# Transposing activations two chunks at a time through one PSUM bank

## What is computed

```
layer(h):                       # twice, with weights of its own
    a    = softmax(h @ h.T / sqrt(D)) * adj ;  attn = a / (sum(a) + 1e-10)
    ctx  = (attn above diagonal) @ (h @ wl.T + bl) + diag(attn) * (h @ ws.T + bs)
         + (attn below diagonal) @ (h @ wr.T + br)
    h    = relu(layernorm(ctx, 1e-12) * g + beta)
y   = layernorm(x + layer(layer(x)))
out = layernorm(y + attention(y, adj, 12 heads, + 0.1 * adj on the scores, masked where adj == 0))
```

## Time and profile before

| | |
|---|---|
| median of 3 runs | 1866.24 us (1865.49 to 1866.89) |
| the profiled execution | 1864.76 us, its span 1863.0 us |
| mean granted TensorE clock | 0.977 |
| instructions | 39868 |

### The profile page before, as it was taken

One profiled execution on the slowest core, in us unless ns is written; L12 is line 12 of the kernel. 1 busy time (PEld: TensorE's weight loads), 2 busy tenths in 40 slices (PEclk: granted clock), 3 DMA queues, 4 the chain that ended last, 5 costly groups with the idle time before them and its releaser, 6 DMA issues.

```text
span 1863.0 us, 39868 instructions
## 1 busy us (share of the span) xinstructions
PE 1731.2 (93%) x13120; PEld 1633.3 (88%) x13120; DVE 1555.4 (83%) x5383; ACT 1267.5 (68%) x3036; POOL 652.9 (35%) x777
## 2 busy tenths in 40 slices
PE   4899999999999999999999999999999999999963
PEld 4799899999999999999999999899999999999952
DVE  4578889888888988888998888898888889888865
ACT  3466767676767776676767676676767776767644
POOL 1223333343333334343334333333434333433331
PEclk9899999999999999999999999999999999999975
DMA  5157666767666666766676776666666667677555
GB/s 156 29 106 149 127 130 131 145 135 147 145 122 132 136 143 141 150 134 125 132 144 139 143 144 124 129 137 145 138 151 136 123 135 140 138 143 144 115 116 116
DMA packets 550036, 247.65 MB, mean 133 GB/s; under 512 B 423100, under 2 KB 549832, under 8 KB 549832
## 3 DMA queue, kind: packets, MB, share of 16 engines
q1 hardware_dynamic: 538928, 231.91, 61.9%
q10 hardware_dynamic: 10904, 13.20, 2.1%
HBM read 56.25 MB, written 12.58 MB: 37 GB/s over the span
## 4 chain that ended last, share of the span: by engine, by line
PE 61%; DVE 24%; ACT 9%; issue 3%; DMA 1%; SPq 1%; ACTq 0%; POOL 0%; DVEq 0%; POOLq 0%
PE bank_w L384 33%; PE bank_m L384 10%; PE bank_u L384 6%; PE bank_o L384 4%; DVE halves L890 4%; DVE bank_s L885 4%; PE bank_s L384 4%; ACT normed L632 2%; ACT bank_s L683 2%; DVE stats_y L851 2%; ACT halves L692 2%; DVE hlrl L792 2%; DVE normed L848 2%; PE bank_t L401 2%; DVE attTl L797 1%
## 5 line engine op out<-in xcount | busy, mean ns | idle before, releaser
L683 ACT ACTIVATE bank_s<-bank_s,hmin 128x256 f32<-128x256 f32 x768 | 311.1, 445 | 129.8 <-DVE hmin L885 114.1
L885 DVE CUSTOM_DVE_ANT_0 bank_s<-bank_s,bias_adj 128x256 f32<-128x256 f32 x768 | 308.1, 446 | 40.7 <-PE bank_s L384 40.4
L890 DVE TENSOR_TENSOR halves<-bank_s,halves 128x512 f16<-128x512 f32 x384 | 262.3, 683 | 27.4 <-ACT halves L692 24.3
L692 ACT ACTIVATE halves<-bank_s 128x512 f16<-128x512 f32 x384 | 228.6, 596 | 4.2
L384 PE MATMUL bank_w<-w_graph0h,hT_ach 128*128 128x384 f32 x576 | 201.5, 350 | 10.3 <-DVE w_graph0l L745 6.0
L384 PE MATMUL bank_w<-w_graph1h,hT_bh 128*128 128x384 f32 x576 | 200.1, 347 | 0.0
L384 PE MATMUL bank_o<-v_parts,pT 128*128 128x99 bf16 (+1 forms) x3072 | 186.7, 204 | 12.6 <-DMA pT<-halves 9.3
L384 PE MATMUL bank_w<-w_graph0l,hT_ach 128*128 128x384 f32 x576 | 195.6, 340 | 0.0
L384 PE MATMUL bank_w<-w_graph0h,hT_acl 128*128 128x384 f32 x576 | 195.3, 339 | 0.0
L384 PE MATMUL bank_w<-w_graph1l,hT_bh 128*128 128x384 f32 x576 | 195.0, 339 | 0.0
L384 PE MATMUL bank_w<-w_graph1h,hT_bl 128*128 128x384 f32 x576 | 194.6, 338 | 0.0
(11 more groups left out here) (177 smaller groups left out, 5327.3 us busy)
## 6 DMA issues: line engine op xcount, KB each, us to landing
x_in<-in_x SPq DMA_DIRECT2D x64, 384.0 KB, 3.7
adj_in<-in_adj SPq DMA_DIRECT2D x96, 256.0 KB, 3.6
q_st<-qk_hi SPq DMA_DIRECT2D x256, 96.0 KB, 2.3
k_st<-qk_hi SPq DMA_DIRECT2D x256, 96.0 KB, 2.3
q_st<-qk_lo SPq DMA_DIRECT2D x128, 96.0 KB, 2.2
k_st<-qk_lo SPq DMA_DIRECT2D x128, 96.0 KB, 2.2
out<-result ACTq DMA_DIRECT2D x32, 384.0 KB, 3.8
pT<-halves SPq DMA_TRANSPOSE x384, 3.1
```

The costliest lines, as they stand in the source:

```text
L683: nc.scalar.activation(bank[:, i * S:(i + 1) * S], bank[:, i * S:(i + 1) * S], ACT.Exp, bias=hmin[:, i, k:k + 1], scale=-1.0).then_inc(s_p ...
L692: nc.scalar.activation(halves[:, k % SPLIT, :, 0, :], bank_s[k % 2][:, :].rearrange("p (i s) -> p i s", i=NT), ACT.Copy).then_inc(s_pt_hi, 1)
L885: ve.tensor_tensor_reduce(bank_s[k % 2][:, i * S:(i + 1) * S], bank_s[k % 2][:, i * S:(i + 1) * S], bias_adj[:, i, :], -SCALE, BIG, ALU.ad ...
L890: ve.tensor_tensor(halves[:, k % SPLIT, :, 1, :], bank_s[k % 2][:, :].rearrange("p (i s) -> p i s", i=NT), halves[:, k % SPLIT, :, 0, :], ...
```

## The change

The three tensors are turned in two steps in place of three: TURNS = ((0, 1), (2,)). Step 0 does chunks 0 and 1, four transposes that fill bank_t wholly; step 1 does chunk 2 with two transposes. For x and y ACT copies and DVE subtracts 512 columns in one instruction for step 0, 256 for step 1. For h ACT still makes two passes per chunk (its scale and bias differ by chunk), four for step 0, and then DVE subtracts 512 columns in one. All semaphore counts on these steps go from NC to len(TURNS). In the lists the first of the three steps goes away, the second becomes step 0, the third step 1, and the rest keeps its place: on PE `turn_y.0` stands ahead of `a_mix.0` and `turn_y.1` behind it, `turn_h.0` ahead of v.0 and `turn_h.1` between v.0 and v.1, `turn_x.0` behind `b_scores` and `turn_x.1` behind `b_proj.1`. The waits in a_x, b_x, a_scores, b_scores, a_proj, b_proj and qk change in their counts only, and they mean the same as before.

```diff
+TURNS = ((0, 1), (2,))
...
@@ -47,26 +48,26 @@
 ORDER = {
     "pe": """
         a_proj.2-1 scores.7-1 a_proj.3-1 attend.4-1 a_proj.4-1 a_proj.5-1 attend.5-1 scores.8-1 scores.9-1
-        turn_y.0-1 turn_y.1-1 a_mix.0-1 turn_y.2-1 attend.6-1 scores.10-1 a_mix.1-1 attend.7-1 q.0 q.1
-        scores.11-1 attend.8-1 q.2 k.0 attend.9-1 turn_h.0 k.1 k.2 turn_h.1 v.0 turn_h.2 v.1 attend.10-1
-        turn_x.0 attend.11-1 b_scores.0 turn_x.1 scores.0 scores.1 b_proj.0 b_proj.1 turn_x.2 b_proj.2
+        turn_y.0-1 a_mix.0-1 turn_y.1-1 attend.6-1 scores.10-1 a_mix.1-1 attend.7-1 q.0 q.1
+        scores.11-1 attend.8-1 q.2 k.0 attend.9-1 k.1 k.2 turn_h.0 v.0 turn_h.1 v.1 attend.10-1
+        attend.11-1 b_scores.0 turn_x.0 scores.0 scores.1 b_proj.0 b_proj.1 turn_x.1 b_proj.2
         scores.2 b_proj.3 b_turn.0 b_proj.4 b_proj.5 scores.3 scores.4 a_scores.0 b_mix.0 attend.0 scores.5
         attend.1 b_mix.1 a_proj.0 a_proj.1 attend.2 a_turn.0 scores.6 attend.3""",
     "act": """
         a_proj.2-1 scores.7-1 weights.6-1 a_proj.3-1 b_norm2.0-1 a_proj.4-1 weights.7-1 b_out.0-1 a_proj.5-1
-        turn_y.0-1 scores.8-1 turn_y.1-1 weights.8-1 scores.9-1 turn_y.2-1 weights.9-1 scores.10-1 q.0
-        h_norm.0 q.1 weights.10-1 h_apply.0 q.2 scores.11-1 k.0 weights.11-1 turn_h.0 k.1 k.2 turn_h.1
-        turn_h.2 v.0 turn_x.0 v.1 turn_x.1 scores.0 b_proj.0 weights.0 b_scores.0 b_proj.1 scores.1 weights.1
-        turn_x.2 b_proj.2 b_proj.3 scores.2 weights.2 b_turn.0 c_norm.0 b_proj.4 b_proj.5 c_apply.0 c_store.0
+        scores.8-1 turn_y.0-1 weights.8-1 scores.9-1 turn_y.1-1 weights.9-1 scores.10-1 q.0
+        h_norm.0 q.1 weights.10-1 h_apply.0 q.2 scores.11-1 k.0 weights.11-1 k.1 k.2 turn_h.0
+        turn_h.1 v.0 v.1 turn_x.0 scores.0 b_proj.0 weights.0 b_scores.0 b_proj.1 scores.1 weights.1
+        turn_x.1 b_proj.2 b_proj.3 scores.2 weights.2 b_turn.0 c_norm.0 b_proj.4 b_proj.5 c_apply.0 c_store.0
         scores.3 weights.3 a_scores.0 scores.4 b_norm.0 weights.4 a_proj.0 b_apply.0 a_proj.1 scores.5
         weights.5 a_turn.0 scores.6""",
     "dve": """
         scores.7-1 b_resid.0-1 b_resid.1-1 b_norm2.0-1 weights.6-1 b_out.0-1 a_turn.0-1 weights.7-1 a_proj.4-1
-        scores.8-1 a_proj.5-1 turn_y.0-1 attend.5-1 scores.9-1 turn_y.1-1 weights.8-1 a_mix.0-1 scores.10-1
-        turn_y.2-1 weights.9-1 a_mix.1-1 h_norm.0 attend.7-1 q.0 h_apply.0 q.1 scores.11-1 weights.10-1 q.2
-        k.0 weights.11-1 turn_h.0 k.1 attend.9-1 k.2 turn_h.1 turn_h.2 attend.11-1 turn_x.0 v.0 scores.0 v.1
-        b_scores.0 turn_x.1 b_proj.0 weights.0 scores.1 b_proj.1 b_mask.0 scores.2 c_stat.1 weights.1 c_stat.0
-        c_norm.0 turn_x.2 weights.2 b_turn.0 c_apply.0 scores.3 b_proj.4 b_proj.5 scores.4 a_scores.0
+        scores.8-1 a_proj.5-1 attend.5-1 scores.9-1 turn_y.0-1 weights.8-1 a_mix.0-1 scores.10-1
+        turn_y.1-1 weights.9-1 a_mix.1-1 h_norm.0 attend.7-1 q.0 h_apply.0 q.1 scores.11-1 weights.10-1 q.2
+        k.0 weights.11-1 k.1 attend.9-1 k.2 turn_h.0 turn_h.1 attend.11-1 v.0 scores.0 v.1
+        b_scores.0 turn_x.0 b_proj.0 weights.0 scores.1 b_proj.1 b_mask.0 scores.2 c_stat.1 weights.1 c_stat.0
+        c_norm.0 turn_x.1 weights.2 b_turn.0 c_apply.0 scores.3 b_proj.4 b_proj.5 scores.4 a_scores.0
         weights.3 b_mix.0 a_mask.0 b_mix.1 b_norm.0 attend.1 b_apply.0 weights.4 scores.5 a_proj.0 a_proj.1
         attend.3 weights.5 scores.6""",
     "pool": """
...
 
+        def turned(hT, k):
+
+            return hT[:, TURNS[k][0]:TURNS[k][-1] + 1, :].rearrange("p c s -> p (c s)")
+
         def run(steps, todo):
             for name, k, at in todo:
                 if name in steps:
...
             def turn_x(t, k):
                 pe.wait_ge(s_xa, 16 * (t + 1))
-                wait(pe, s_th_lo, NC * t) if k == 0 else None
-                wait(pe, s_tx_lo, NC * t + k)
-                for i in range(NT):
-                    last = nc.tensor.transpose(bank_t[:, i * P:(i + 1) * P], x_in[:, i, k * P:(k + 1) * P], ident[:, :])
+                wait(pe, s_th_lo, len(TURNS) * t) if k == 0 else None
+                wait(pe, s_tx_lo, len(TURNS) * t + k)
+                for n, c in enumerate(TURNS[k]):
+                    for i in range(NT):
+                        last = nc.tensor.transpose(bank_t[:, n * S + i * P:n * S + (i + 1) * P],
+                                                   x_in[:, i, c * P:(c + 1) * P], ident[:, :])
                 last.then_inc(s_tx_pe, 1)
 
             def turn_h(t, k):
                 pe.wait_ge(s_h1, NT * t)
                 if k == 0:
-                    wait(pe, s_ty_lo, NC * (t - 1))
-                    pe.wait_ge(s_tx_lo, NC * t)
-                wait(pe, s_th_lo, NC * (t - 1) + k)
-                for i in range(NT):
-                    last = nc.tensor.transpose(bank_t[:, i * P:(i + 1) * P], normed[:, i, k * P:(k + 1) * P], ident[:, :])
+                    wait(pe, s_ty_lo, len(TURNS) * (t - 1))
+                    pe.wait_ge(s_tx_lo, len(TURNS) * t)
+                wait(pe, s_th_lo, len(TURNS) * (t - 1) + k)
+                for n, c in enumerate(TURNS[k]):
+                    for i in range(NT):
+                        last = nc.tensor.transpose(bank_t[:, n * S + i * P:n * S + (i + 1) * P],
+                                                   normed[:, i, c * P:(c + 1) * P], ident[:, :])
                 last.then_inc(s_th_pe, 1)
 
             def turn_y(t, k):
                 pe.wait_ge(s_y, NT * t)
                 if k == 0:
-                    pe.wait_ge(s_th_lo, NC * t)
+                    pe.wait_ge(s_th_lo, len(TURNS) * t)
                     if t != NB:
-                        pe.wait_ge(s_tx_lo, NC * (t + 1))
-                wait(pe, s_ty_lo, NC * (t - 1) + k)
-                for i in range(NT):
-                    last = nc.tensor.transpose(bank_t[:, i * P:(i + 1) * P], y_in[:, i, k * P:(k + 1) * P], ident[:, :])
+                        pe.wait_ge(s_tx_lo, len(TURNS) * (t + 1))
+                wait(pe, s_ty_lo, len(TURNS) * (t - 1) + k)
+                for n, c in enumerate(TURNS[k]):
+                    for i in range(NT):
+                        last = nc.tensor.transpose(bank_t[:, n * S + i * P:n * S + (i + 1) * P],
+                                                   y_in[:, i, c * P:(c + 1) * P], ident[:, :])
                 last.then_inc(s_ty_pe, 1)
 
...
             def turn_x(t, k):
-                act.wait_ge(s_tx_pe, NC * t + k + 1)
+                act.wait_ge(s_tx_pe, len(TURNS) * t + k + 1)
                 if k == 0:
                     wait(act, s_v, NT * (t - 1))
-                nc.scalar.activation(hT_ac[0][:, k, :], bank_t[:, 0:S], ACT.Copy).then_inc(s_tx_hi, 1)
+                nc.scalar.activation(turned(hT_ac[0], k), bank_t[:, 0:len(TURNS[k]) * S], ACT.Copy).then_inc(s_tx_hi, 1)
 
             def turn_y(t, k):
-                act.wait_ge(s_ty_pe, NC * (t - 1) + k + 1)
+                act.wait_ge(s_ty_pe, len(TURNS) * (t - 1) + k + 1)
                 if k == 0 and t != NB:
                     act.wait_ge(s_proj, 6 * layer_a(t) + 6)
-                nc.scalar.activation(hT_ac[0][:, k, :], bank_t[:, 0:S], ACT.Copy).then_inc(s_ty_hi, 1)
+                nc.scalar.activation(turned(hT_ac[0], k), bank_t[:, 0:len(TURNS[k]) * S], ACT.Copy).then_inc(s_ty_hi, 1)
 
             def turn_h(t, k):
 
-                act.wait_ge(s_th_pe, NC * (t - 1) + k + 1)
-                for dst in (hT_b[0][:, k, :], bank_t[:, 0:S]):
-                    nc.scalar.activation(dst, bank_t[:, 0:S], ACT.Relu, bias=b1_col[:, k:k + 1],
-                                         scale=g1_col[:, k:k + 1]).then_inc(s_th_f, 1)
+                act.wait_ge(s_th_pe, len(TURNS) * (t - 1) + k + 1)
+                for n, c in enumerate(TURNS[k]):
+                    for dst in (hT_b[0][:, c, :], bank_t[:, n * S:(n + 1) * S]):
+                        nc.scalar.activation(dst, bank_t[:, n * S:(n + 1) * S], ACT.Relu, bias=b1_col[:, c:c + 1],
+                                             scale=g1_col[:, c:c + 1]).then_inc(s_th_f, 1)
 
...
             def turn_x(t, k):
-                dve.wait_ge(s_tx_hi, NC * t + k + 1)
-                ve.tensor_tensor(hT_ac[1][:, k, :], bank_t[:, 0:S], hT_ac[0][:, k, :], ALU.subtract).then_inc(s_tx_lo, 1)
+                dve.wait_ge(s_tx_hi, len(TURNS) * t + k + 1)
+                ve.tensor_tensor(turned(hT_ac[1], k), bank_t[:, 0:len(TURNS[k]) * S], turned(hT_ac[0], k), ALU.subtract).then_inc(s_tx_lo, 1)
 
             def turn_y(t, k):
-                dve.wait_ge(s_ty_hi, NC * (t - 1) + k + 1)
-                ve.tensor_tensor(hT_ac[1][:, k, :], bank_t[:, 0:S], hT_ac[0][:, k, :], ALU.subtract).then_inc(s_ty_lo, 1)
+                dve.wait_ge(s_ty_hi, len(TURNS) * (t - 1) + k + 1)
+                ve.tensor_tensor(turned(hT_ac[1], k), bank_t[:, 0:len(TURNS[k]) * S], turned(hT_ac[0], k), ALU.subtract).then_inc(s_ty_lo, 1)
 
             def turn_h(t, k):
```

(16 more changed lines are left out.)

## The result

The changed kernel takes 1891.5 us (median; 1889.7 to 1893.2), the kernel before, run beside it, 1866.1 us. The ratio is 1.0136, with an interval of 1.0123 to 1.015: slower by 1.4%, 25.4 us, where 1889 us was predicted, with a range of 1878 to 1903. The profiled execution has a span of 1890.9 us and a mean granted clock of 0.974.

The account below looks back on a forecast made before the run. Neither PE nor DVE alone was taken as the bound, but a chain through both. 30 periods at +0.95 us plus 0.8 gave +29.3; less 4.5 and 2, +22.8 us: 1889 us, range 1878 to 1903.

Parts of the forecast that it names:

- turn_y: Transposes of y_in: PE's wait goes but DVE's queue is late, so only 0.06 us a period gained, bounds 0 and 0.15.
- turn_h: Between v.0 and v.1: four ACT passes make PE wait 1.39 us at turn_h.1, 1.08 us late against before.
- turn_x: Around b_scores: 0.27 us gained where the pair between the attends goes, 0.18 lost to four transposes behind b_scores.
- Cover on DVE: Behind scores.0: DVE's 0.27 us more ahead of b_proj's subtractions is covered by 0.38 us idle ahead of weights.2.
- Late k copies: Ahead of scores: PE's 6.6 us idle, read as late stacked copies of k, absorbs 4.5 us, bounds 3 and 6.6.
- The steady sum: All periods together: 29.3 us of delay less 4.5 us for late copies, 24.8 us slower.
- Start and end: Start, first turn_h and last turn_y: two hand-overs for three take off 2 us together, bounds 1 and 3.
- The rule weighed: Skill's 125 ns overhead per DVE instruction: three merges would save 0.38 us a period rather than 0.18, some 6 us lower.
- The hand-over hides: Rival, chance 0.14: PE not held at turn_h.1 beyond its lead, even at 2.36 us; wholly hidden about 1854 us.
- covers gone: Rival, chance 0.16: DVE's extra 0.27 us counts in full and late copies stay late, +36 us, 1902 us.
- It comes out even: Rival, chance 0.06: waits shift into unseen slack or time lost anyway to stacked copies and DMA, within 3.7 us of 1866.

Follow-up runs that it names:

- e4: Kernel before with only turn_x in two steps, x alone merged: 1865.5 us, ratio 0.9994.
- e7: Changed kernel with turn_h.1 on PE moved from between v.0 and v.1 to behind v.1: 1893.3 us, ratio 1.0147.
- e1: Changed kernel with turn_h back to three steps at its old places, x and y in two: 1862.0 us, ratio 0.9979.
- e10: e7 with turn_x.0's subtraction on DVE moved ahead of b_scores.0 (maximum and two-element product): 1880.3 us, ratio 1.0097.
- e6: Changed kernel without ACT's second pass over the bank in turn_h, for timing only, results not valid: 1864.3 us, ratio 0.9995.
- e8: e7 with b_scores.0 on DVE moved ahead of v.1's subtraction: 1908.0 us, ratio 1.023.

## Why the prediction was right

The forecast was the likeliest case: the merged groups save little where DVE is late anyway, and `turn_h` costs a wait. By its own steps, with before and after in the same quiet period, counted from `turn_y.0` on PE:

| step | offset before | after | shift | forecast |
|---|---|---|---|---|
| `a_mix.1` | 4.46 | 4.31 | -0.15 | -0.06 (0 to -0.15) |
| k.1 | 12.10 | 11.93 | -0.17 | -0.06 |
| v.0 | 14.96 | 14.54 | -0.42 | -0.31 |
| last `turn_h` | 16.64 | 17.60 | +0.96 | +1.08 |
| `b_scores` | 19.34 | 20.05 | +0.71 | +0.81 |
| scores.0 | 21.70 | 22.63 | +0.93 | +0.99 |
| period | 54.82 | 55.74 | +0.92 | +0.95 |

- **turn_y.** Right in kind: 1.3 us of wait went and little was gained. The gain is the upper bound I gave, 0.15 and not 0.06: the two subtractions' saving of 0.06, and the 0.09 by which DVE had waited for PE at `a_mix.0` (0.69 us between two starts for 0.60). I had named that gap and left it out of the value. `a_mix.0` waits for DVE's hlrl, as forecast, although the sums of waits name POOL's cut: it starts 0.10 us after the end of hlrl in all 31 periods.
- **turn_h.** From the start of the four transposes to `turn_h.1` I had worked out 3.44 us. It is 3.41 (998.31 to 1001.72): 0.63 to ACT's first pass, 1.90 for the four, 0.04 to the subtraction, 0.69 for it, 0.15 to PE. PE is ready at 998.66 + 1.69 = 1000.35 and waits 1.37 us, for 1.39. The profile's own figure, 1.22, is smaller since it counts the wait from the end of the last matmul, which overlaps the next start.
- **turn_x.** The pair between the attends was worth 0.25 (0.96 to 0.71) for 0.27, and the wide group behind `b_scores` cost 0.22 (0.71 to 0.93) for 0.18. The two cancel. e4 puts `turn_x` alone at -0.05 us a period.
- **Cover on DVE.** Behind scores.0 the delay stays at 0.92 to 0.93 until the next `turn_y`, so DVE's 0.27 us more in front of `b_proj` were hidden, as forecast. e7 shows that this cover is thin: with PE 0.26 us earlier and DVE held longer, DVE binds there.
- **Late k copies.** On PE the distance from the matmul ahead of scores.0 to scores.0 is 0.03 us in most periods; what it has above that comes to 4.5 us in all periods together before, and to 0.1 after: 4.4 us absorbed, for 4.5. That it is k's copies that came late is not shown, as the profile names no releaser there.
- **The steady sum.** From the first `turn_y` to the last PE takes 1704.5 us before and 1728.5 after, +24.0; forecast 29.3 - 4.5 = 24.8.
- **Start and end.** The 2 us that I took off for them don't show. In this pair of executions the stretch before the first `turn_y` is 3.1 us longer and that after the last 0.7 longer. The first `turn_y` of the changed kernel and of e1 to e10 lies anywhere between 87.4 and 91.1 us, without order by what they change, so one execution can't tell 2 us there. By the medians, 25.4 in all, the rest beside the 24.0 is +1.4 and not -2. This is the only term with the wrong sign, 3.4 us off, more than the whole difference between 1889 and 1891.5. The steady sum, 0.8 us too high, makes up for a part of it.

**The rule weighed.** A DVE subtraction of 512 columns for two of 256 saves 0.13 us of duration (0.69 for 2 x 0.41), and 0.06 us of DVE's queue, which moves on by the distance between starts (0.60 for 2 x 0.33). The Trainium skill (Perfetto Trace Analysis, section Optimizing Scalar/DVE Operations) puts the overhead of an instruction at about 125 ns for DVE on PSUM, as engine-busy time, and says that the latency in the profile is about twice that. The trace has about half of both. The estimate by the page, 6 us less, would have given 1883, and the kernel takes 1891.5. The section's other half says that breaking up instructions may let work finish sooner where ACT and DVE aren't saturated but cause bubbles on others. That is what e1 against the changed kernel shows: `turn_h` in three steps for two, 0.9979 for 1.0136.

**The rivals.** "The hand-over hides" had its point at 2.36 us from the transposes to `turn_h.1`. e6, with two passes left out, has 16.74 - 14.21 = 2.53 us and comes out at 54.87 us a period, 0.05 over before, just on the slow side of that point. The "covers gone" rival wanted more than 56 us a period, and there were 55.74. "It comes out even" is 25 us away.

## What to carry to other kernels

When transposes or copies are merged to save instructions, look at the hand-over and not at the count: with passes that can't be merged, it grows by their full length, and the work that covered the narrow one no longer does. Put the widest group where the most work of the waiting engine stands behind it (here last, 4.3 us of cover), and the narrow one where the cover is short: the whole change then gains 0.67% in place of losing 1.36%. A large wait of the busiest engine may be worth only what the releasing engine's queue gets shorter by: here 43.6 us of waits held 4.4. And when the sums of waits name a releaser, look at the times: the one named here had been done 0.85 us before the engine went on.

## What the runs showed of the hardware

A tiny DVE operation can be held for as long as a large one of POOL's. DVE's TENSOR_SCALAR on two elements per partition, from SBUF to SBUF, takes 0.17 us where none of POOL's large operations on `result` runs (one case of 0.36 in e10 apart), and beside its additions 0.47 (changed kernel), 0.99 (e7), 0.50 (e8) and 0.41 us (e10) in most periods. In each of these four kernels it starts 30 times during such an addition, and by the single records of the trace it ends 0.02 to 0.03 us after that addition does, every time. The kernel before has the hold too, mostly 0.31 to 0.33 us and there mostly beside POOL's product ahead of the additions. In the same stretches DVE's operations on PSUM kept their usual durations: the maximum over bank_u 0.68 us, the subtraction from bank_t 0.68. The Trainium skill (SBUF — State Buffer, section Who interferes with whom) says that DVE and GpSimd share a pair of SBUF ports as an exclusive lock, that DVE's tensor_scalar can take it in its two-port modes, and that the one which comes second blocks fully until the other is done. The trace agrees, with 0.17 to 0.99 us; whether the product ran in such a mode no run shows. I had not expected it for two elements, and in e7 it cost as much as the move could gain, 9 us by the ratios of e7 and e10.
